# Last part of a vision tower on one core: the layer norm's variance summed onto all partitions by one product, the root over 256 columns

## The reference

```python
h = x
for blk in range(3):
    i0, i1 = (2 * blk, 2 * blk + 1)
    y = _qlora_linear(h, qweights[i0], scales[i0], biases[i0], lora_a[i0], lora_b[i0])
    y = _layernorm(y, ln_gamma[blk], ln_beta[blk])      # (y - mean) * rsqrt(var + 1e-5) * g + b
    y = jax.nn.gelu(y, approximate=False)
    y = _qlora_linear(y, qweights[i1], scales[i1], biases[i1], lora_a[i1], lora_b[i1])
    h = y + h
```

## Time and profile before

| | |
|---|---|
| median of 3 runs | 506.34 us (504.92 to 506.62) |
| the profiled execution | 505.93 us, its span 504.1 us |
| mean granted TensorE clock | 0.878 |
| busy in the span: PE, DVE, ACT, POOL | 396.7, 308.7, 240.8, 153.7 us |
| the last part | about 424 us to the end of the span |

### The profile page before, as it was taken

One profiled execution on the slowest core, in us unless ns is written; L12 is line 12 of the kernel. 1 busy time (PEld: TensorE's weight loads), 2 busy tenths in 40 slices (PEclk: granted clock), 3 DMA queues, 4 the chain that ended last, 5 costly groups with the idle time before them and its releaser, 6 DMA issues.

```text
span 504.1 us, 9608 instructions
## 1 busy us (share of the span) xinstructions
PE 396.7 (79%) x3584; PEld 285.0 (57%) x3584; DVE 308.7 (61%) x841; ACT 240.8 (48%) x508; POOL 153.7 (30%) x192
## 2 busy tenths in 40 slices
PE   5788877767698998999999974649931337799997
PEld 4566654555587874444466952234420235689996
DVE  2989878889573721222332276696899978446642
ACT  4345544456655411222221125961895867656561
POOL 4388773689611250000000361700100002214310
PEclk9999999899989998999999995755555558999999
DMA  8961111692007023011110144000000000000002
GB/s 257 381 222 18 20 24 26 248 427 82 3 0 280 25 90 115 22 42 44 43 42 22 52 125 204 1 4 0 1 0 0 3 4 2 0 1 1 1 22 78
DMA packets 18513, 36.95 MB, mean 73 GB/s; under 512 B 2424, under 2 KB 14916, under 8 KB 17060
## 3 DMA queue, kind: packets, MB, share of 16 engines
q1 hardware_dynamic: 17540, 33.85, 19.5%
q0 software_dynamic: 928, 2.49, 1.5%
HBM read 29.19 MB, written 5.90 MB: 70 GB/s over the span
## 4 chain that ended last, share of the span: by engine, by line
PE 50%; DVE 19%; ACT 11%; issue 9%; POOL 8%; DMA 2%; SPq 1%; DVEq 0%; ACTq 0%; POOLq 0%
PE psum L1404 9%; PE psum L1406 5%; PE psum L2533 5%; PE psum L2566 3%; PE psum L1036 2%; POOL front L1353 2%; POOL expert_rows L1346 2%; PE psum L2572 2%; PE psum L1444 2%; ACT experts L1836 2%; PE psum L2550 1%; PE psum L2399 1%; PE psum L2398 1%; PE psum L1461 1%; PE psum L908 1%
## 5 line engine op out<-in xcount | busy, mean ns | idle before, releaser
L1404 PE MATMUL psum<-experts,ring 128*64 x128 | 46.3, 505 | 0.6 <-ACT ring L1553 0.6
L1405 PE MATMUL psum<-experts,ring 128*64 128x512 f32 (+1 forms) x128 | 46.3, 505 | 0.0
L1353 POOL DMA_INDIRECT front<-expert_results,slot_of x10 | 9.9, 987 | 102.7 <-DMA expert_results<-ring 99.9
L1205 DVE TENSOR_TENSOR ring<-ring,psum 128x512 f32<-128x512 f32 x13 | 8.9, 688 | 50.4 <-PE psum L1405 34.2
L1444 PE MATMUL psum<-front,shared 128*128 128x256 f32 (+1 forms) x160 | 34.6, 370 | 0.0
L2533 PE MATMUL psum<-experts 128*128 128x256 f32 (+1 forms) x120 | 27.5, 372 | 4.6 <-ACT experts L2596 4.6
L1444 PEld LDWEIGHTS psum<-front,shared 128*128 128x128 f32 x160 | 29.2, 190 | 3.2
L1404 PEld LDWEIGHTS psum<-experts,ring 128*64 128x64 f32 x128 | 16.6, 140 | 22.3 <-issue 18.9
L654 PE MATMUL psum<-experts,ring 128*128 128x256 f32 x108 | 25.1, 382 | 3.5 <-DVE experts L508 1.5
L1406 PE MATMUL psum<-experts,ring 128*128 x80 | 27.7, 487 | 0.0
L2533 PEld LDWEIGHTS psum<-experts 128*128 128x128 f32 x120 | 21.8, 190 | 7.6 <-ACT experts L2596 5.4
(11 more groups left out here) (379 smaller groups left out, 1110.1 us busy)
## 6 DMA issues: line engine op xcount, KB each, us to landing
experts<-in_experts SPq DMA_DIRECT2D x8, 1536.0 KB, 12.8
experts<-in_x SPq DMA_DIRECT2D x9, 384.0 KB, 9.1
expert_rows<-zeros SPq DMA_DIRECT2D x1, 1664.0 KB, 14.3
ring<-expert_rows SPq DMA_DIRECT2D x26, 64.0 KB, 2.2
shared<-in_shared SPq DMA_DIRECT2D x1, 1536.0 KB, 17.4
experts<-in_ffn_q SPq DMA_DIRECT2D x1, 1536.0 KB, 6.3
experts<-in_ffn_s SPq DMA_DIRECT2D x1, 1536.0 KB, 9.6
experts<-in_pos_embed SPq DMA_DIRECT2D x1, 1152.0 KB, 10.7
```

The costliest lines, as they stand in the source:

```text
L1353: nc.gpsimd.indirect_dma_start(moved[0:n, t, :], None, ys_dram, bass.IndirectOffsetOnAxis(ap=slot_of[0:n, t:t + 1], axis=0)).then_inc(rows ...
L1404: nc.tensor.matmul(out[0:HALF, :], rows[:, 0:HALF], slot_w(t, block, k, n), **flags)
L1405: return nc.tensor.matmul(out[HALF:P, :], rows[:, HALF:P], own_w(t, block, k, n), **flags)
```

## The change

The sum over the partitions becomes one product of the 128x128 matrix of ones with the joined squares: every partition gets the sums of all 256 (192) tokens of the chunk, on the free axis. The variance (DVE) and the power (POOL) then work on 128x256 and not 128x2; the second input of the power is one column, broadcast. The spread products, their semaphore and their PSUM banks go; `normed` reads the factor from `ffn_rs` in SBUF. The two tiles `ffn_var` and `ffn_rs` become views of the region `front`. POOL's power of step n now waits for `normed(n-2)`, where before it waited for `spread(n-2)`.

```diff
-        ffn_var = sb("ffn_var", [P, 2, 2])
-        ffn_rs = sb("ffn_rs", [P, 2, 2])
+        ffn_var = view(front, 0, 2, CHUNK)
+        ffn_rs = view(front, 2 * CHUNK, 2, CHUNK)
...
-                nc.vector.tensor_scalar(ffn_var[:, n % 2, :], psum[:, 2 + n % 2, 0:2], 1.0 / D, LN_EPS, ALU.mult, ALU.add).then_inc(ffn_var_ready.sem, 1)
+                w = FFN_CHUNKS[n % NC][1]
+                nc.vector.tensor_scalar(ffn_var[:, n % 2, 0:w], psum[:, 2 + n % 2, 0:w], 1.0 / D, LN_EPS, ALU.mult, ALU.add).then_inc(ffn_var_ready.sem, 1)
...
-                dve.wait_ge(ffn_spread.sem, ffn_spread.done(n))
-                rs = psum[:, 4 + n % 2, 0:w].rearrange("p (o c) -> p o c", o=1).to_broadcast((P, KD, w))
+                dve.wait_ge(ffn_rs_ready.sem, ffn_rs_ready.done(n))
+                rs = ffn_rs[:, n % 2:n % 2 + 1, 0:w].to_broadcast((P, KD, w))
                 nc.vector.tensor_tensor(y, y, rs, ALU.mult).then_inc(ffn_normed.sem, 1)
...
-                    pool.wait_ge(ffn_spread.sem, ffn_spread.done(n - 2))
-                nc.gpsimd.tensor_tensor(ffn_rs[:, n % 2, :], ffn_var[:, n % 2, :], minus_half[:, 0:2], ALU.pow).then_inc(ffn_rs_ready.sem, 1)
+                    pool.wait_ge(ffn_normed.sem, ffn_normed.done(n - 2))
+                w = FFN_CHUNKS[n % NC][1]
+                nc.gpsimd.tensor_tensor(ffn_rs[:, n % 2, 0:w], ffn_var[:, n % 2, 0:w], minus_half[:, 0:1].to_broadcast((P, w)), ALU.pow).then_inc(ffn_rs_ready.sem, 1)
...
-                for u in range(2):
-                    mm = nc.tensor.matmul(psum[:, 2 + n % 2, u:u + 1], ffn_sq[n % 2][:, 0, u * P:(u + 1) * P], ones[:, 0:1], start=True, stop=True)
-                mm.then_inc(ffn_summed.sem, 1)
-
-            def spread(n):
-                pe.wait_ge(ffn_rs_ready.sem, ffn_rs_ready.done(n))
-                if n >= 2:
-                    pe.wait_ge(ffn_normed.sem, ffn_normed.done(n - 2))
-                for u, (_, m) in enumerate(tiles_of_chunk(n % NC)):
-                    mm = nc.tensor.matmul(psum[:, 4 + n % 2, u * P:u * P + m], ffn_rs[:, n % 2, u:u + 1].to_broadcast((P, P)), ident[:, 0:m],
-                                          start=True, stop=True)
-                mm.then_inc(ffn_spread.sem, 1)
+                w = FFN_CHUNKS[n % NC][1]
+                nc.tensor.matmul(psum[:, 2 + n % 2, 0:w], ones, ffn_sq[n % 2][:, 0, 0:w], start=True, stop=True).then_inc(ffn_summed.sem, 1)
...
-                if 0 <= i - 2 < STEPS:
-                    spread(i - 2)
```

More of the change, by code:

```diff
@@ L2371, in tower @@
         ffn_summed, ffn_var_ready = Count("ffn_summed", o_quant, NT // 2), Count("ffn_var_ready", o_y_ready, NT // 2)
-        ffn_rs_ready, ffn_spread = Count("ffn_rs_ready", sl_hT_ready, SLOT_TILES), Count("ffn_spread", sl_down, SLOT_TILES)
+        ffn_rs_ready = Count("ffn_rs_ready", sl_hT_ready, SLOT_TILES)
         ffn_normed, ffn_gelu = Count("ffn_normed", sl_y_ready, SLOT_TILES), Count("ffn_gelu", sh_down, NT // 2)
```

## The result

The changed kernel takes 1037.22 us (median of 4 runs, 1034.54 to 1042.31) where the kernel before takes 506.21 (median of 4): a ratio of 2.0511, 95% interval 2.042 to 2.0601. The direction was forecast, the size was not: 963 us, with a range that ended at 1012. The profiled execution has a span of 1036.5 us.

A forecast was written before the change was run, and what follows sets the result against it. PE bound the kernel before; POOL would after. First power at 432.25 us, plus powers 480, additions 6.4, gaps 28 and tail 14, made a 960.7 us span; 1.8 more gave 962.5, say 963 us, range 600 to 1012.

The forecast's parts named there:

- POOL becomes the bound: On POOL, the 15 widened powers alone were to take 480 us, where PE needed about 60.
- The step: On POOL, each 256-column power was to take 33.7 us, against PE's present step of 4.35 us.
- the lost PE clock: On PE, idle most of the time, the clock was expected at 1.2 GHz instead of 2.4 GHz.
- the waits on DVE: On DVE, waits ended by POOL were to last some 30 us each.
- The break-even price: On POOL, 0.015 us a column, below which a 256-column power stays under PE's present step of 4.35 us.
- the power's price per column: On POOL, each further column of a power was to cost 0.13 us (0.12 to 0.14), 33.7 us for 256.
- The gaps: Between POOL's powers, 14 gaps of 2.0 us for DVE work locked out during a power, 28 us.
- rival 4: No lock between POOL's power and DVE: 28 us less, shorter tail, about 930 us; chance 0.2 of the likeliest case's 0.66.
- The tail: At the kernel's end, 14 us (11 to 16), with PE's products doubled and perhaps one more chunk held back.
- PE's 5.9 us: On PE's path, spreads and old column sums go (6.9 + 4.0 us), new sums cost 5.0: 5.9 us less.
- DVE at nothing: On DVE, the wider variance adds some 0.26 us a step, costing nothing while PE or POOL sets the step.
- Rivals 1, 2 and 3: Power's columns: 1 stream like additions, 500 us, chance 0.12; 2 overlap, 726/608 us, 0.17; 3 cost 0.53 us each, 0.05.

## Why the prediction missed

**POOL becomes the bound: right.** The step, the direction, the lost PE clock and the waits on DVE came as said. The break-even price of 0.015 us a column was passed tenfold.

**The term that was mis-sized: the power's price per column.** The step "the second column costs 0.13 us (0.12 to 0.14 by the choice of row)" failed. It is 0.157 to 0.159 us by the run of many widths, 0.15 to 0.16 between the narrowest. 255 further columns and 15 steps stand behind each hundredth: 12 x 255 + 3 x 191 = 3633 columns, so 0.01 us is 36 us. The powers took 588 us for 480. The page's durations of the earlier trace rows, 0.550 and 0.692, gave 0.142, nearer than the starts that I preferred, and outside the stated 0.12 to 0.14. The rows shown have one column at 0.53 to 0.56 us and two at 0.66 to 0.69, so the ends should have been 0.10 and 0.16, and at 0.16 the top of the range would have been 1084 us and not 1012.

**The gaps: wrong, and in the other direction.** The 28 us did not come. The stretched joinings beside an addition were carried over to a power, whose hold on DVE is 0.41 us of 41, and the variance of the next chunk was always in hand. For the gaps that was rival 4, given 0.2.

**The tail: 9.9 us for 14.** No chunk was held back; PE's last second product took 2.08 + 0.85 + 1.27 + 0.45 = 4.65 us by the chain. Only its first tile, 2.08 + 0.85, was about double the 0.87 + 0.44 of the earlier trace rows, at a granted clock of 0.50; by the second the clock was rising (0.81 from 1031.2 to 1032.5 us), and it took 1.72 us where the last tile before had taken 1.46.

Put together: 960.7 + 108 (powers) - 28 (gaps) - 4 (tail) = 1036.7 us, and the span is 1036.5. The errors partly hid each other: with the gaps gone and the tail as measured, the same price of 0.13 would have forecast 931, so the forecast was nearer than its main term deserved.

**PE's 5.9 us: right.** The product in the power's place gave 6.3 us by the medians, with an interval that holds 5.9 (by its own terms the new sums are 4.9 and not 5.0 us, and the gain 6.0). **DVE at nothing: right**; the wide variance took 0.425 us for the 0.42 read, and the normalising product, left at 0.687, took 1.295 beside POOL's work, which cost nothing where POOL set the step. **Rivals 1, 2 and 3:** the widths exclude the first two at every width tried; of the third only the number came true, a price above 0.14 us, which the prediction gave 0.05: its reason, 0.53 us for every column, is excluded by the same rows, and waits of a wide operand's own by the straight line.

## What to carry to other kernels

Before an operation is widened on an engine that looks free, take its marginal price for a column and compare it with the price at which that engine becomes the bound; here a tenth of the price would have been the limit. A price that is multiplied by hundreds must come from widths in the same place and far apart, and its range from how far such rows scatter. Two narrow widths are not enough even in the same place: the 0.152 us between one and two columns would still give 39.3 us for 256 columns, 1.8 short of what they take. One kernel with many widths settles it in a single run. Where the bound engine's work is the aim, look for a cheaper form on that engine first: two bf16 parts took more than half off the spread for two narrow operations more on POOL, which PE did not wait for.

## What was not expected of the hardware

A power on POOL costs 0.157 to 0.159 us for each column of 128 partitions, in a straight line from 2 to 256 columns, with a broadcast exponent as with a full tile of them, beside some 0.4 us once. A two-input addition costs 0.0021, a seventy-fifth.

POOL's power holds up a DVE instruction with two SBUF inputs for 0.41 us at 256 columns and 0.19 at 128, at its start alone; after that both run side by side. A DVE product that is already running holds up the power in turn (41.57 us for 41.12).
